# A four-layer sequence model: the first layer cut in two, its scan set beside two attentions, its preparation beside the last layers

## The chip, the core and the metric

One core of one Trainium2 chip. The metric is the device time of one execution in microseconds (us), lower is better. One core works through eight independent sequences of 512 rows by 128 columns, one after the other; nothing is exchanged with other cores. Engine names are those of the profile: PE (TensorE), DVE (VectorE), ACT (ScalarE), POOL (GpSimd), SP (SyncE, which here only issues transfers).

## The reference, cut to what matters

The input is x, eight sequences of 512x128 in float32. Each goes through four pairs of layers; a layernorm stands before each layer and a residual is added after it:

```python
# pair 0: a two-way selective scan (Mamba), then 16 experts of width 64, top 2 of 16 in groups
xc    = silu(causal_conv(xi))                    # 256 channels, forward and reversed
delta = softplus(dt @ dtproj_w.T + dtproj_b)
h     = exp(delta * A) * h + (delta * xc) * B    # over 512 positions, 16 states a channel
y     = ((h * C).sum(states) + D * xc) * silu(z) # both directions averaged, projected, added to x
# pair 1: attention, 16 heads of 64 with a relative bias, then 8 low-rank experts
# pair 2: attention, 16 heads of 8, rotary, causal; then a layer that begins with a second
#         16-head attention of 8 (rotary, not causal) and ends with 8 experts of width 512
# pair 3: a memory layer (8 recurrences), then 8 gated experts of width 256
```

The scan of one sequence is 2 directions x 2 halves of the channels x 16 states = 64 steps, each a first-order recurrence on a 128x512 tile.

## The kernel before, in words

All tiles are 128 partitions by 512 columns. Most stages are blocks with a barrier between them. The order of one pass (`layers`, L1495 to L2029) is: `moe0`, `attn1`, `lora1`, `attn2` (causal), `attn3`, and then the stage `slot`. Inside `slot` two streams share all engines: `mamba` (L669 to L958), which does the whole first layer of the **next** sequence, and `last_layers` (L1275), which does the rest of this one (ln1, experts 2, ln2, ln3, memory, ln4, experts 3). The first sequence's first layer runs alone in a stage `first`; the last pass (names that begin with z) has no first layer beside it. The passes but the last are one hardware loop (`Fori`) of seven.

How two streams are merged is written out by hand. Each stream is a generator per engine that yields a due time before each piece; `in_turn` (L583) always takes the stream with the earlier due time. So the order on each engine is fixed when the program is built, and an engine that waits for a semaphore holds back all that stands behind it, of both streams. The due times are only ranks; the true pace is set by the waits.

One scan step m is five instructions: PE broadcasts row B into a PSUM bank (L769, `DRIVE`, three banks), DVE multiplies it by `du` (L935), ACT makes the decay (L839), DVE scans (L942), POOL multiplies by row C (L859), PE adds the product into `SUM` (L777). SP loads row C, spread over the partitions, into one of three buffers (L726). In the order of DVE the product of step s stands ahead of the scan of step s-1:

```python
yield SCAN + STEP * s + 0.4
V.tensor_tensor(DRIVE[s % 3], DRIVE[s % 3], du[:, d, t, :], ALU.mult)          # step s
V.tensor_tensor_scan(work[:, m % RW, :], decay[m % RD], DRIVE[m % 3], 0.0, ...) # m = s - 1
```

What comes before the scan (norms, projection, convolution, softplus, rows B and C; L730 to L910) is called the preparation here. Its tiles and the scan's share SBUF.

A 16-head attention (`rope_attention`, `head8_attention`, L367 to L576, `project_back`) is: norm, projection, rotary and splitting into bf16 parts on DVE, then 93 steps in which PE makes the scores S of a tile (L426), DVE takes its row maximum (L550 causal, L553 not), and, 20 steps later, PE makes them again transposed (T), ACT takes the exponential (L524), POOL masks the diagonal in the causal one (L533), and PE weighs the values (L485). S and T tiles go through a ring of six PSUM banks (`RING`, L378), transposes and sums have banks 6 and 7 to themselves. All weights lie in SBUF (`WF`).

## Time and profile before

| | |
|---|---|
| median of 3 runs | 5811.86 us (5811.77 to 5815.04) |
| the profiled execution's own time | 5812.37 us |
| its span, first to last instruction | 5810.6 us |
| granted TensorE clock, mean over the span | 0.844 |
| busy share PE, DVE, ACT, POOL | 77%, 65%, 53%, 20% |

Busy time of an engine is counted once where its instructions overlap. The clock is the share of full speed that TensorE was granted: 0.5 is 1.2 GHz and 1.0 is 2.4 GHz. In a window row the engines stand in the order PE, PEld (weight loads), DVE, ACT, POOL. In a timeline or lines row what stands in brackets or behind the second bar is idle time of the engine just before, and what released it.

### The profile page before, as it was taken

To read this page: it belongs to the slowest core of one execution; us is meant where nothing else is said; L and a number is where in the kernel's file an instruction comes from. 1 tells how busy PE (TensorE), PEld (TensorE's weight loads), DVE (VectorE), ACT (ScalarE), POOL (GpSimd) and SP (SyncE) were. 2 spreads that over 40 slices of the span, in tenths; PEclk is the share of its full clock that TensorE was granted. 3 is DMA by queue.
4 is the path that set the end of the run, shared out by engine and by line. 5 is a ranking of instruction groups with operands and counts; after the bars stand their busy time and mean duration, and the time that the engine had idled before them with its cause. 6 is when DMAs were issued, how large, how long until landed. Compare 5 with 4: busy or idle time off the path is not lost. (4 is left out here: it accounts for less than half of the span.)

```text
span 5810.6 us, 67170 instructions
## 1 busy us (share of the span) xinstructions
PE 4485.7 (77%) x20516; PEld 2226.2 (38%) x20516; DVE 3772.0 (65%) x8877; ACT 3064.0 (53%) x5351; POOL 1140.3 (20%) x1356
## 2 busy tenths in 40 slices
PE   5786778877788777887778777788778877788777
PEld 2342434424344243442434324343243433444334
DVE  6756586565865658656686556865668555686554
ACT  3365645556455555555655556555565555555443
POOL 2401132011320123201231012310123111231100
PEclk8996989978898788987889878897789987899778
DMA  4210021100210002100121001210012100121000
GB/s 160 87 36 1 21 65 55 32 1 25 67 55 26 1 28 71 52 22 1 34 73 47 20 1 37 75 48 13 1 42 75 46 11 1 44 73 47 7 1 2
DMA packets 104076, 218.53 MB, mean 38 GB/s; under 512 B 11072, under 2 KB 19776, under 8 KB 103152
## 3 DMA queue, kind: packets, MB, share of 16 engines
q1 hardware_dynamic: 103680, 213.81, 11.6%
q8 instruction: 180, 2.95, 0.2%
q14 instruction: 216, 1.77, 0.1%
HBM read 211.08 MB, written 2.69 MB: 37 GB/s over the span
## 5 line engine op out<-in xcount | busy, mean ns | idle before, releaser
L859 POOL TENSOR_TENSOR slot_work<-slot_work,slot_c_all 128x512 f32<-128x512 f32 x448 | 570.2, 1273 | 1015.9 <-DVE slot_work L942 1015.0
L777 PE MATMUL BANKS<-slot_work,WF 128*128 128x512 f32 x896 | 530.5, 679 | 5.7 <-DVE slot_du L918 2.9
L524 ACT ACTIVATE attn_prob<-BANKS 128x512 f32<-128x512 f32 (+3 forms) x896 | 401.5, 532 | 122.5 <-PE BANKS L426 119.0
L1000 PEld LDWEIGHTS BANKS<-WF,slot_x_a 128*128 128x128 f32 x2688 | 359.3, 197 | 264.5 <-ACT slot_x_a L1040 133.5
L1000 PE MATMUL BANKS<-WF,slot_x_a 128*128 128x128 f32 x2688 | 373.3, 283 | 86.3 <-ACT slot_x_a L1040 86.3
L1010 PE MATMUL BANKS<-XT,WF 128*128 128x512 f32 x768 | 425.3, 639 | 2.6 <-ACT slot_comb_t L306 2.6
L769 PE MATMUL BANKS<-slot_bcs,WB 96*128 96x512 bf16 x448 | 189.1, 422 | 305.1 <-DVE slot_work L942 304.0
L202 POOL TENSOR_TENSOR rstd<-rstd,WF 128x4 f32<-128x4 f32 x40 | 40.3, 1007 | 1572.7 <-DVE rstd L220 1559.5
L1809 DVE CUSTOM_DVE_ANT_0 attn_biased<-BANKS,attn_toep 128x512 f32<-128x512 f32 x448 | 306.0, 684 | 51.9 <-PE BANKS L1707 46.6
L1788 ACT COPY attn_probt<-BANKS 128x512 f32<-128x512 f32 x448 | 261.0, 583 | 147.3 <-PE BANKS L1714 144.4
L426 PE MATMUL BANKS<-attn_parts_kT,attn_parts_qT 64*128 64x512 bf16 (+3 forms) x896 | 309.2, 437 | 33.6 <-ACT attn_parts_qT L504 20.7
L935 DVE TENSOR_TENSOR BANKS<-BANKS,slot_du 128x512 f32<-128x512 f32 x448 | 307.6, 687 | 36.0 <-PE BANKS L769 33.4
L942 DVE TENSOR_TENSOR_SCAN slot_work<-slot_decay,BANKS 128x512 f32<-128x512 f32 x273 | 329.7, 1208 | 0.0
L1780 ACT ACTIVATE attn_prob<-attn_biased,attn_nmax 128x512 f32<-128x512 f32 x448 | 326.9, 730 | 1.3 <-DVE attn_nmax L1809 1.2
L553 DVE TENSOR_REDUCE attn_nmax<-BANKS 128x1 f32<-128x512 f32 x448 | 282.0, 683 | 67.9 <-PE BANKS L426 65.6
L1714 PE MATMUL BANKS<-WF,attn_prob 128*128 128x128 f32 x1792 | 280.3, 281 | 7.6 <-ACT attn_probt L1788 4.3
L550 DVE CUSTOM_DVE_ANT_0 attn_masked<-BANKS,WF 128x128 f32<-128x128 f32 (+1 forms) x448 | 202.1, 489 | 127.4 <-PE BANKS L426 126.6
L1714 PEld LDWEIGHTS BANKS<-WF,attn_prob 128*128 128x128 f32 x1792 | 190.9, 140 | 243.9 <-DVE attn_prob L1816 157.0
L1707 PE MATMUL BANKS<-attn_qk 64*128 64x512 f32 x896 | 257.8, 653 | 4.7 <-ACT attn_qk L1762 4.7
L426 PE MATMUL BANKS<-attn_qm,attn_parts_kT 64*128 64x512 bf16 (+3 forms) x896 | 238.8, 394 | 17.1 <-ACT attn_qm L510 11.3
L1814 DVE RECIPROCAL attn_rden<-attn_den 128x1 f32<-128x1 f32 x448 | 72.1, 161 | 275.3 <-ACT attn_prob L1780 272.3
L485 PE MATMUL BANKS<-attn_prob,attn_vals 128*32 128x512 f32 (+3 forms) x1792 | 226.1, 580 | 16.9 <-ACT attn_prob L524 10.7
(674 smaller groups left out, 9464.7 us busy)
## 6 DMA issues: line engine op xcount, KB each, us to landing
slot_c_all<-c_rows SPq DMA_DIRECT2D x448, 256.0 KB, 3.1
attn_toep<-bias_line SPq DMA_DIRECT2D x112, 448.0 KB, 4.4
first_c_all<-c_rows SPq DMA_DIRECT2D x64, 256.0 KB, 3.1
WF<-in_wf SPq DMA_DIRECT2D x4, 1964.0 KB, 16.2
zattn_toep<-bias_line SPq DMA_DIRECT2D x16, 448.0 KB, 4.3
WF<-in_wf SPq DMA_DIRECT2D x3, 800.0 KB, 17.2
WF<-in_wf SPq DMA_DIRECT2D x3, 785.5 KB, 6.0
XIN<-in_x SPq DMA_DIRECT2D x8, 256.0 KB, 2.9
```

Source lines behind the costliest of these rows:

```text
L426: nc.tensor.matmul(bank(kind, i), left[rows, P * tile:P * (tile + 1)], right[rows, lo:hi], start=True, stop=True).then_inc(sem, 1)
L524: nc.scalar.activation(prob[:, i % PR, lo:hi], bank("T", i), ACT.Exp).then_inc(exped, 1)
L553: V.tensor_reduce(nmax[:, j, h:h + 1], bank("S", s), AX.X, ALU.max, negate=True).then_inc(maxed, 1)
L777: nc.tensor.matmul(SUM, ident, work[:, m % RW, :], start=(n == 0), stop=(n == NS - 1)).then_inc(acc, 1)
L859: nc.gpsimd.tensor_tensor(work[:, m % RW, :], work[:, m % RW, :], c_all[:, m % RC, :], ALU.mult).then_inc(rd, 1)
L935: V.tensor_tensor(DRIVE[s % 3], DRIVE[s % 3], du[:, d, t, :], ALU.mult).then_inc(drv, 1)
L942: V.tensor_tensor_scan(work[:, m % RW, :], decay[m % RD], DRIVE[m % 3], 0.0, ALU.mult, ALU.add).then_inc(scn, 1)
L1000: last = nc.tensor.matmul(DOWN[e % 2][:, j * D:(j + 1) * D], a1[:, i % 3, j * P:(j + 1) * P], w_down[:, i * D:(i + 1) * D], start=(t == 0 ...
L1010: last = nc.tensor.matmul(place("up", i), w_up[:, i * P:(i + 1) * P], XT[:, :], start=True, stop=True)
L1714: last = nc.tensor.transpose(bank[:, kt * P:(kt + 1) * P], prob[:, u % NP_, kt * P:(kt + 1) * P], ident)
L1780: nc.scalar.activation(prob[:, e % NP_, :], biased[:, e % NS_, :], ACT.Exp, bias=nmax[:, e:e + 1], scale=-1.0, accum_out=den[:, e:e + 1]). ...
L1809: V.tensor_tensor_reduce(biased[:, s % NS_, :], PS[s % NS_], toep[:, h % 4, c:c + SEQ], -1.0, BIG, ALU.add, ALU.min, nmax[:, s:s + 1]).the ...
```

## The change

- `mamba` becomes `mamba_pre` (the preparation) and `mamba_scan`. What passes between them (`M_KEPT`) lives in SBUF all the time; a tile `XM` takes the scan's result.
- The stages `attn2`, `attn3` and `slot` become two: `heads`, where the scan for sequence b+1 runs beside both 16-head attentions, and `last`, where the preparation for b+2 runs beside the last layers. The start is `p0`, `s0`, `p1`: preparation and scan of sequence 0, preparation of sequence 1, each alone. The loop is six passes, then a pass y (scan, no preparation) and a pass z (neither).
- The attentions become merged streams with due times (`rope_parts`, `head8_parts`, `back_parts`, which issue the same arithmetic). Banks 0 to 2 are the scan's; S, T and all transposes share a ring of four banks (3 to 6), taken in a fixed order, and bank 7 sums the weighed values.
- The scan has two `DRIVE` banks for three, four decay buffers for five, six work buffers for eight; each step's scan follows its own product. One step is due each 2.8 attention steps, from due time 4.0 (1.95 and alone in `s0`).
- The weights of experts 2 are no longer in SBUF: SP loads them expert by expert, 512 KB each, into a ring of three.
- `last_layers` copies `XM` to `X`; experts 3 have other due times (3.0 for 5.2).

```diff
     XTM = sbt(top, "XTM", [P, SEQ])
+    XM = sbt(top, "XM", [P, NJ, D])
+    M_KEPT = (sbt(top, "m_zs", [P, ND, SEQ]), sbt(top, "m_xc", [P, 2, ND, SEQ]), sbt(top, "m_delta", [P, 2, ND, SEQ]),
+              sbt(top, "m_du", [P, 2, ND, SEQ]), sbt(top, "m_bcs", [96, 2, SEQ], BF16))
...
-    def head8_attention(st, parts, vals, causal, O):
...
-        RING = 6
...
-    def mamba(st, after=None):
...
-        RD, RW, RC, AHEAD, FLUSH = 5, 8, 3, 5, 4
-        PRE, SCAN, STEP = 13.5, 52.0, 2.6
-        TAIL = SCAN + STEP * STEPS
...
+    def mamba_pre(st, fetch):
+        PRE = 13.5
+        zs, xc, delta, du, bcs = M_KEPT
...
-        SUM, DRIVE, OUT = PS[0], (PS[1], PS[2], PS[3]), PS[1]
...
         def sync(sp):
+            yield -3.0
+            sp.dma_start(XIN[:, :, :], fetch()).then_inc(xin_ld, 16)
...
+            yield 52.0
+            sp.wait_ge(cput, 32)
...
+    def mamba_scan(st, dest, START, STEP):
+        STEPS = 2 * ND * NS
+        RD, RW, RC, LATE = 4, 6, 3, 2
+        TAIL = START + STEP * STEPS
+        zs, xc, delta, du, bcs = M_KEPT
...
+        b_cast, dec, drv, scn, rd, acc = (st.sem(n) for n in ("b_cast", "dec", "drv", "scn", "multiplied", "acc"))
...
+        SUM, DRIVE, OUT = PS[0], (PS[1], PS[2]), PS[1]
...
+        def sync(sp):
+            for m in range(STEPS):
+                d, _, n = step(m)
+                yield at(m - 3)
+                if m >= RC:
+                    sp.wait_ge(rd, m - RC + 1)
+                row = c_dram[d, n:n + 1, :]
+                src = bass.AP(row.tensor, row.offset, [[0, P], [1, SEQ]])
+                sp.dma_start(c_all[:, m % RC, :], src).then_inc(c_ld[m % RC], 16)
...
+        def tensor(pe):
+            for s in range(STEPS + LATE):
+                if s < STEPS:
+                    d, _, n = step(s)
+                    yield at(s) - 1.0
+                    if s >= 2:
+                        pe.wait_ge(scn, s - 1)
+                    row = WBF("pick", 96)[:, n:n + 1]
+                    nc.tensor.matmul(DRIVE[s % 2], bc(row, [96, P]), bcs[:, d, :], start=True, stop=True).then_inc(b_cast, 1)
+                m = s - LATE
+                if m >= 0:
+                    n = m % NS
+                    yield at(s) + 0.45 * STEP
+                    pe.wait_ge(rd, m + 1)
+                    if n == 0 and m:
+                        pe.wait_ge(emptied, m // NS)
+                    nc.tensor.matmul(SUM, ident, work[:, m % RW, :], start=(n == 0), stop=(n == NS - 1)).then_inc(acc, 1)
...
+                d, t, n = step(m)
+                yield at(m - 2) + 0.3 * STEP
+                if m >= RD:
+                    act.wait_ge(scn, m - RD + 1)
+                a = (d * ND + t) * NS + n
+                nc.scalar.activation(decay[m % RD], delta[:, d, t, :], ACT.Exp, scale=W("A")[:, a:a + 1]).then_inc(dec, 1)
+        def gpsimd(pool):
+            for m in range(STEPS):
+                yield at(m) + 0.9 * STEP
+                pool.wait_ge(scn, m + 1)
+                pool.wait_ge(c_ld[m % RC], 16 * (m // RC + 1))
+                nc.gpsimd.tensor_tensor(work[:, m % RW, :], work[:, m % RW, :], c_all[:, m % RC, :], ALU.mult).then_inc(rd, 1)
...
-            for s in range(STEPS + 1):
-                yield SCAN + STEP * s + 0.4
-                if s < STEPS:
-                    d, t, n = step(s)
-                    dve.wait_ge(b_cast, s + 1)
-                    if s % (ND * NS) == 0:
-                        dve.wait_ge(dud, d + 1)
-                    V.tensor_tensor(DRIVE[s % 3], DRIVE[s % 3], du[:, d, t, :], ALU.mult).then_inc(drv, 1)
-                m = s - 1
-                if m >= 0:
...
+            for s in range(STEPS):
+                d, t, n = step(s)
+                yield at(s)
+                dve.wait_ge(b_cast, s + 1)
+                V.tensor_tensor(DRIVE[s % 2], DRIVE[s % 2], du[:, d, t, :], ALU.mult).then_inc(drv, 1)
+                if s >= NS and n == LATE:
+                    yield at(s) + 0.2 * STEP
                     flush(s // NS - 1)
-            yield TAIL + STEP * (AHEAD + 1) + 1.0
+                yield at(s) + 0.5 * STEP
+                dve.wait_ge(drv, s + 1)
+                dve.wait_ge(dec, s + 1)
+                if s >= RW:
+                    dve.wait_ge(acc, s - RW + 1)
+                V.tensor_tensor_scan(work[:, s % RW, :], decay[s % RD], DRIVE[s % 2], 0.0,
+                                     ALU.mult, ALU.add).then_inc(scn, 1)
+            yield TAIL + STEP * LATE + 1.0
             flush(2 * ND - 1)
...
-            V.tensor_tensor(X[:, :, :], XIN[:, :, :], OUT.rearrange(tiles, j=NJ), ALU.add)
+            V.tensor_tensor(dest[:, :, :], XIN[:, :, :], OUT.rearrange(tiles, j=NJ), ALU.add)
...
+        def sync(sp):
+            for e in range(E if stream is not None else 0):
+                yield at - 10.0 if e < RW else at + 0.2 + step * tiles_per * (e - RW + 1)
+                if e >= RW:
+                    sp.wait_ge(used, tiles_per * (e - RW + 1))
+                sp.dma_start(ring_w[:, e % RW, :], stream[e]).then_inc(w_ld[e % RW], 16)
...
                 yield at + 0.2 + step * i
-                last = nc.tensor.matmul(place("up", i), w_up[:, i * P:(i + 1) * P], XT[:, :], start=True, stop=True)
+                if stream is not None and i % tiles_per == 0:
+                    pe.wait_ge(w_ld[i // tiles_per % RW], 16 * (i // tiles_per // RW + 1))
...
+                                 FF // P, comb2, comb2_t, Y, 7.4, 2.0, stream=w2)
         ln2 = norm_parts(st, "ln2", Y, XN, SMALL, 73.0, gain=W("g2"), shift=W("be2_2"))
...
-                                 W("b2_3", E3), E3, HID // P, comb3, comb3_t, XO, 138.0, 5.2)
+                                 W("b2_3", E3), E3, HID // P, comb3, comb3_t, XO, 138.0, 3.0)
...
             nc.vector.tensor_tensor(XO[:, :, :], X[:, :, :], XN[:, :, :], ALU.add).then_inc(freed, 1)
+            if copy_next:
+                dve.wait_ge(freed, 1)
+                nc.vector.tensor_copy(X[:, :, :], XM[:, :, :])
             for layer in (ln3, memo, ln4, moe3):
...
+    def rope_parts(st, tag, ready, w_qkv, bias, half, tiles4, banks, at, again):
...
+    def head8_parts(st, tag, rope, tiles4, causal, O, ring, wbank, at, u):
...
+            return at + u * s
+        order = [("turn", n) for n in range(4)]
+        for s in range(N + LAG + 8):
+            if s < N:
+                order += [("S", s)] + [("turn", s)] * (4 <= s < H)
+            if s % PER == 2 and 1 <= s // PER <= NGR:
+                order.append(("Q", s // PER - 1))
+            if 0 <= s - LAG < N:
+                order.append(("T", s - LAG))
+            i = s - LAG - 7
+            if 0 <= i < N and i % PER == PER - 1:
+                order.append(("O", i // PER))
+        slot = {item: n for n, item in enumerate(order)}
+        done = {"S": maxed, "T": exped, "turn": ev, "Q": q_moved, "O": o_normed}
...
+        def tensor(pe):
+            def take(kind, i):
+                n = slot[kind, i] - len(ring)
+                if n >= 0:
+                    pe.wait_ge(done[order[n][0]], order[n][1] + 1)
+                return bank(kind, i)
...
+                    if causal:
+                        V.tensor_tensor_reduce(got, got, W("early")[:, SEQ - hi:], -1.0, BIG,
+                                               ALU.add, ALU.min, nmax[:, j, h:h + 1]).then_inc(maxed, 1)
+                    else:
+                        V.tensor_reduce(nmax[:, j, h:h + 1], got, AX.X, ALU.max, negate=True).then_inc(maxed, 1)
...
+    def back_parts(st, tag, heads, O, turned_o, w_o, add_to, banks, at, bias=None):
...
+    def both_attentions(st, at, u):
+        RING, WEIGH = PS[3:7], PS[7]
...
+        for tag, w_qkv, bias, half, causal, w_o, add_to, bias_o in (
+                ("a2", W("qkv2"), None, False, True, W("o2"), X, None),
+                ("a3", W("qkv3"), W("bqkv3"), True, False, W("o3"), XN, W("bo3"))):
+            ln = norm_parts(st, f"{tag}_ln", X, XN, SMALL, at, dst_t=XT, banks=(RING[1], RING[0]), after=before)
+            rope = rope_parts(st, tag, ln.ready, w_qkv, bias, half, raw, RING, at + 6.0, bool(layers))
+            head = head8_parts(st, tag, rope, heads, causal, O, RING, WEIGH, at + 26.0, u)
+            back = back_parts(st, f"{tag}_pb", head, O, ot[:, 0, :], w_o, add_to, RING, head.end + 0.5, bias=bias_o)
+            layers += [ln, rope, head, back]
+            at, before = head.end + 4.5, (back.added, 1)
...
-    with Stage("first", last=True) as st:
-        layer = mamba(st)
+    with Stage("p0") as st:
+        layer = mamba_pre(st, lambda: one(xs, 0))
         with nc.Block() as block:
             run(block, layer)
...
+    with Stage("s0") as st:
+        layer = mamba_scan(st, X, 2.0, 1.95)
+        with nc.Block() as block:
+            run(block, layer, clear=True)
+        release_stale()
+    with Stage("p1", last=True) as st:
+        layer = mamba_pre(st, lambda: one(xs, 1))
+        with nc.Block() as block:
...
+    def layers(b, scan_next, pre_next):
...
-        def rope_attention(st, w_qkv, bias, half, causal, O):
...
-        def project_back(st, tag, O, w_o, add_to, bias=None):
...
-        with Stage("slot", last=True, at_end=store) as st:
-            taken = st.sem("x_taken")
-            streams = [mamba(st, after=(taken, 1))] if ahead else []
-            streams.append(last_layers(st, taken))
+        with Stage("heads", last=True) as st:
+            streams = [mamba_scan(st, XM, 4.0, 2.8)] if scan_next else []
...
+            streams.append(both_attentions(st, 0.0, 1.0))
             with nc.Block() as block:
-                run(block, *streams, first=clear)
...
-    with nc.Fori(0, out.shape[0] - 1) as b:
-        layers(b, True)
+        with Stage("last", last=True, at_end=store) as st:
+            streams = [mamba_pre(st, lambda: one(xs, b + 2))] if pre_next else []
+            streams.append(last_layers(st, scan_next))
+            with nc.Block() as block:
+                run(block, *streams)
+    n = out.shape[0]
+    with nc.Fori(0, n - 2) as b:
+        layers(b, True, True)
+    prefix[0] = "y"
+    layers(n - 2, True, False)
     prefix[0] = "z"
-    layers(out.shape[0] - 1, False)
+    layers(n - 1, False, False)
```

## Rows read from the trace of the kernel before

**Rows 1.** The page: busy time and share of each engine; costliest group, line 859

```profile
PE 4485.7 (77%) x20516; PEld 2226.2 (38%) x20516; DVE 3772.0 (65%) x8877; ACT 3064.0 (53%) x5351; POOL 1140.3 (20%) x1356
L859 POOL TENSOR_TENSOR slot_work<-slot_work,slot_c_all 128x512 f32<-128x512 f32 x448 | 570.2, 1273 | 1015.9 <-DVE slot_work L942 1015.0
```

**Rows 2.** Windows by stage: from:to, length, busy and count per engine, clock, DMA, GB/s

```profile
225.60:424.00 198.40, 175.90 (x860) 92.56 (x860) 118.59 (x366) 115.83 (x253) 19.09 (x13) 0.92 0.13 39
424.00:613.40 189.40, 132.09 (x784) 50.65 (x784) 111.00 (x327) 98.83 (x204) 28.61 (x80) 0.72 0.00 1
613.40:940.50 327.10, 247.04 (x912) 132.71 (x912) 240.44 (x412) 174.04 (x217) 95.27 (x76) 0.87 0.17 53
5623.50:5807.50 184.00, 141.61 (x668) 91.17 (x668) 84.57 (x217) 58.31 (x85) 4.04 (x4) 0.84 0.00 1
```

**Rows 3.** Windows, the two 16-head attentions of the first pass in five pieces

```profile
424.00:447.00 23.00, 7.65 (x20) 4.03 (x20) 12.59 (x31) 7.04 (x17) 4.35 (x6) 0.57 0.01 1
447.00:509.90 62.90, 51.16 (x360) 18.93 (x360) 34.28 (x154) 37.32 (x87) 18.26 (x64) 0.74 0.00 1
509.90:539.80 29.90, 11.57 (x37) 6.76 (x37) 15.56 (x39) 6.61 (x14) 6.01 (x10) 0.56 0.00 1
539.80:569.30 29.50, 27.03 (x138) 9.96 (x136) 23.18 (x44) 16.73 (x30) 0.00 (x0) 0.59 0.00 1
569.30:609.00 39.70, 32.83 (x228) 9.41 (x226) 23.32 (x50) 31.13 (x58) 0.00 (x0) 0.99 0.00 1
```

**Rows 4.** Timeline, VectorE in the scan by itself: start, length, engine, line, operation

```profile
208.04 0.67 DVE L935 TENSOR_TENSOR BANKS<-BANKS,first_du 128x512 f32<-128x512 f32 x1
208.62 1.21 DVE L942 TENSOR_TENSOR_SCAN first_work<-first_decay,BANKS 128x512 f32<-128x512 f32 x1
209.74 0.67 DVE L935 TENSOR_TENSOR BANKS<-BANKS,first_du 128x512 f32<-128x512 f32 x1
```

**Rows 5.** Windows, four stretches of the first stage "slot", first layer and last layers together

```profile
613.40:692.80 79.40, 62.48 (x264) 37.83 (x265) 47.91 (x110) 48.14 (x61) 10.86 (x9) 0.86 0.04 11
722.00:757.00 35.00, 19.61 (x52) 8.54 (x51) 29.90 (x62) 14.19 (x22) 10.86 (x9) 0.68 0.15 48
815.00:860.00 45.00, 34.78 (x95) 16.64 (x94) 33.47 (x64) 20.05 (x25) 15.14 (x13) 0.83 0.21 68
860.00:924.00 64.00, 57.53 (x215) 31.02 (x215) 56.47 (x84) 47.11 (x52) 29.94 (x24) 1.00 0.28 89
```

**Rows 6.** Windows, experts alone in the last pass; lines, their gelus within 613.4:692.8

```profile
5631.00:5693.90 62.90, 60.89 (x336) 43.91 (x335) 13.80 (x50) 24.08 (x35) 0.00 (x0) 0.96 0.00 1
L1040 ACT ACTIVATE slot_x_a<-BANKS,WF 128x512 f32<-128x512 f32 x22 | 14.7, 686 | 19.0 <-PE BANKS L1010 18.8
```

**Rows 7.** Timeline, the first VectorE instruction after two stage ends; in brackets the idle time

```profile
225.57 0.68 DVE L215 BATCH_NORM_STATS2 stats<-X 128x6 f32<-128x128 f32 x3 [1.88 <-PEq L136]
940.55 0.68 DVE L215 BATCH_NORM_STATS2 stats<-X 128x6 f32<-128x128 f32 x3 [6.93 <-issue]
```

**Rows 8.** Windows, the first layer alone at the start: preparation, then 64 scan steps

```profile
51.30:101.00 49.70, 23.17 (x39) 6.85 (x39) 34.93 (x65) 20.36 (x25) 7.43 (x7) 0.78 0.01 2
101.00:214.40 113.40, 82.42 (x185) 27.30 (x185) 113.28 (x134) 45.66 (x64) 82.05 (x64) 0.91 0.47 148
```

**Rows 9.** Lines, VectorE at 722:760 beside the scan, and at 5693.9:5724 without it

```profile
L1235 DVE TENSOR_TENSOR slot_mu<-slot_root 128x64 f32<-128x64 f32 x1 | 0.9, 949 | 0.0
L1212 DVE TENSOR_TENSOR slot_qkv<-slot_qkv,slot_parts 128x512 f32<-128x512 f32 x4 | 2.6, 683 | 0.0
L1235 DVE TENSOR_TENSOR zslot_mu<-zslot_root 128x64 f32<-128x64 f32 x1 | 0.2, 224 | 0.0
```

**Rows 10.** The page, DMA issues: tensor, count, KB each, median us to landing

```profile
attn_toep<-bias_line SPq DMA_DIRECT2D x112, 448.0 KB, 4.4
WF<-in_wf SPq DMA_DIRECT2D x3, 785.5 KB, 6.0
XIN<-in_x SPq DMA_DIRECT2D x8, 256.0 KB, 2.9
```

838 lines of the change are left out of this document (412 added, 426 removed).

## The prediction

> **What bounds the kernel now.** I read the page first: DVE 65% and PE 77% of the span, neither full [rows 1]. So the span is a chain of stages with different limits, and the windows by stage are the view that counts [rows 2]. One pass is 198.4 us up to `lora1`, which the change leaves alone, 189.4 us for the two 16-head attentions and 327.1 us from there to the next pass, the stage `slot` with its end. The same last layers without the first layer beside them take 184.0 us. The reader should compare DVE in the four rows: 111.0 us busy of 189.4 in the attentions, 240.4 of 327.1 in `slot`. The scan brings most of the latter: by itself it keeps DVE full (113.28 of 113.40 us) and costs 1.70 us a step, 209.74 less 208.04 [rows 4, 8], so 64 steps are 109 us of DVE wherever they stand. The change moves them to where DVE has 78 us free in 189 and must lengthen that stage, and shortens the other.
>
> **Stage `heads`, with the scan.** Due times place the steps: step s is due at 4+2.8s, an attention's first S at 26, its last step at 119, the second attention's first S at 149.5. That gives 8 scan steps before the first S, 33 in the first attention's steps, 11 between, 12 in the first 34 steps of the second, and none after due time 183. The five pieces of the attentions alone are rows 3. To each I add its scan steps at 1.70 us of DVE:
>
> - before S: 12.6 + 13.6 = 26.2 us of DVE in a piece that took 23.0;
> - first attention: 34.3 + 56.6 = 90.9, took 62.9;
> - between (back projection, norm, rotary): 15.6 + 18.6 = 34.2, took 29.9;
> - first third of the second: 23.2 + 20.5 = 43.7, took 29.5.
>
> Together 195 us of DVE work in pieces that take 145 us now. No engine is ever quite full in a merged stretch, so the question is the share. Three stretches of `slot` bound it: 85% in the norms and splitting of 722 to 757, 74% in 815 to 860, where norm, gate and logits form a chain, and 88% at 860 to 924, where PE was 90% busy too [rows 5]. I take 80% for the two serial pieces (33 and 42 us) and 85 to 88% for the two attention pieces (107 and 49.5 us): 231.5 us, 84% overall. PE comes close but is not the bound: the scan by itself has PE busy 82.4 us in 64 steps, 1.29 each [rows 8]; with the attention's own 51.2 us the largest piece has 94 us of PE at the lower clocks of 0.74 and 0.91, inside 107. ACT has 37 + 24 and POOL 18 + 42 there (0.71 and 1.27 us a step [rows 1, 8]), both covered.
>
> Then the second attention's rest as now, 39.7 us [rows 3], plus 2 for three or four flushes of the sum and the output product that fall there; 3.5 us for the back projection (4.4 now, to 613.4); 2 us for the stage's end, as after `first`, where DVE sat idle 1.88 us [rows 7]. **`heads` is 279 us.** The barriers between the old blocks go, a gain that I leave inside the shares; the smaller ring of four banks I price at nothing in the rest: DVE was busy only 23.3 of those 39.7 us, and the binding engine is PE with 32.8. If PE waits for the older bank more often there, it costs at most one row maximum per four steps, some 9 us of 39.7.
>
> One rule speaks against putting the scan here. DVE work with both inputs in SBUF slows down beside POOL: the small product of line 1235 took 949 ns beside the scan and 224 without [rows 9]. Each rotary part has ten such products and subtractions, and the POOL multiplication that can hold them lasts 1.27 us [rows 1]. At 19 scan steps in the two serial pieces the worst case is 19 x 1.27 = 24 us a pass. Line 1235 lost 0.7 us, while four subtractions of the rotary part's kind (line 1212) kept 683 ns beside the same scan [rows 9]; so I count 2 to 3 us per serial piece, inside the 80%. The Trainium skill ("SBUF — State Buffer", section "Who interferes with whom") says that a DVE instruction with two SBUF inputs and a GpSimd instruction that reads SBUF lock each other out for the whole instruction, whichever starts first. By that rule, the trace agrees for line 1235; that every scan step hits one is the fourth rival.
>
> **Stage `last`, with the preparation.** Until 692.8 the stage `slot` is just this: preparation beside experts 2. In those 79.4 us 22 of 32 tiles had their gelu [rows 5, 6]. Ten remain at 62.9/32 = 1.97 us, 19.7; about 1.5 us of the 79.4 was the scan's beginning. So 97.5 us to the end of experts 2. The rest alone is 5807.5 less 5693.9 = 113.6 us, the copy of X 0.5, and the loop's end 6.9 us of idle DVE [rows 7]. **218.5 us**, against 327.1. The streamed weights: 512 KB lie between the transfers of 448 KB in 4.4 us and of 785.5 KB in 6.0 [rows 10], so about 4.7; a ring of three gives each load the time of some eight tiles, 16 us, and it is hidden. Only the first could be late: it is issued behind XIN (2.9 us) at the stage's start and lands after 7.6 us if alone, and in the last pass the experts began 7.5 us into the stage, at 5631.0 [rows 6]. I cost it at nothing; if the first three loads share the engines it lands with the third, 3 x 4.7 + 2.9 = 17 us in, up to 9.5 us late. SP's waits for rows B and C stand ahead of the loads of experts 6 and 7, which have the same slack. The other due times of experts 3 have no stream to be ranked against.
>
> **The start.** `p0` must now fetch XIN itself: 2.9 + 0.5. `s0` has each scan right behind its own product. They no longer overlap in DVE's pipe: between 0.67 + 1.21 = 1.88 without and 1.70 with full overlap [rows 4] the next product still overlaps the scan before it, so 1.85 a step, 64 x 0.15 = 9.5 us more. A barrier, about 1 us. `p1` is a new 49.7 us of preparation [rows 8], with 3.4 for XIN, 2.5 until POOL's last `du`, and 1 of barrier. Together **70 us** lost once.
>
> **The sum**, against the profiled execution's 5812.4 us (span 5810.6, some 1.8 around it; the median 5811.9 is 0.5 below):
>
> - six loop passes: 189.4 + 327.1 - 279 - 218.5 = 19.0 us each, gain 114;
> - the seventh, with no preparation: 516.5 becomes 279 + 184.0 + 6.9, gain 46.6;
> - the last pass: attentions in one block, gain 3;
> - the start: loss 70.
>
> Net gain 93.5, so 5719; against the median the same within a microsecond. I predict **5720**.
>
> What decides is `heads`. It counts seven times; one microsecond there is 7 us of the time, and the gain is gone at 279 + 93.5/7 = 292.4 us, that is when the shared stretches keep DVE busy below 195/245 = 80%. That is not far from 84%.
>
> **The rivals.** (1) *Tighter overlap*: nothing but exponentials and copies on ACT in `heads`, and PE brought to a higher clock by the scan's matmuls where it now runs at 0.56 to 0.59 [rows 3]. DVE at 93% makes the shared part 210 us, `heads` 257, the time 5720 - 154 = 5566. For it: `slot` already has 88% with PE equally loaded. Against: four banks instead of six.
>
> (2) *The order holds DVE back; slower than before.* PE is two steps ahead of DVE at most: S of step s+2 waits for the maximum of step s, in one queue with the scan's broadcast, its sum and the bursts of eight value products. Each time such a burst falls between two S, DVE runs dry, and the next scan product stands behind the row maximum that is late. At the 74% of 815 to 860 [rows 5] the shared part is 262 us, `heads` 310, the time about 5935. It decides from 80% down, where `heads` passes 292 us.
>
> (3) *The streamed weights arrive late*, the first by 9.5 us in all eight passes and a later one by 1.5: 88 us, 5808, no change. For it only the order on SP's queue; against it the sizes above.
>
> (4) *POOL holds DVE back* for a whole multiplication on every scan step in the serial pieces: 24 - 5 = 19 us a pass more than counted, 5720 + 133 = 5853. For it line 1235, against it line 1212 [rows 9]. The page of the Trainium skill named above would have it wherever the two meet.
>
> That the change doesn't do what it says has one form: the scan is not over midway but its steps lag, since due times are only ranks. It would not; ranks fix the order, and 12 steps before the 34th S is certain.
>
> **Chances.** Forecast 0.55, its own range 5660 to 5790; rival 1 0.20; rival 2 0.17; rival 3 0.05; rival 4 0.03. The range reaches to `heads` of 262 us below, 5600, and 296 us above, 5835; outside lie half of rival 1 and most of rival 2. A difference of 0.2%, 12 us, is about what can be told from no change here. Faster by more: the forecast, rival 1 and a little of the rest, 0.77. Within: 0.04. Slower: rivals 2 and 4 and the forecast's edge, 0.19.
>
> **What would show it.** In the changed profile: windows from the first norm of the attentions to the stage's end of 279 us with DVE about 83% busy and the scan's last step some 225 us in; scan steps 3.1 to 3.4 us apart in the first attention; from there to the next pass 218 us, with the end of experts 2 near 97; `s0` at 1.85 us a step; no idle PE that a weight transfer ends; first `moe0` norm at about 295 us. The prediction is wrong if `heads` exceeds 292 us, or if `last` misses 218 by more than 10.

## The result, and the profile after

| | before | after |
|---|---|---|
| median (runs) | 5811.82 us (4) | 5903.35 us (4, 5894.45 to 5915.09) |
| the profiled execution's own time | 5812.37 us | 5915.09 us |
| its span | 5810.6 us | 5913.4 us |
| ratio of the times, 95% interval | | 1.0159 [1.0139, 1.0179] |

The changed kernel is slower by 91.5 us, 1.6%. 5720 us had been predicted, a gain of 1.6%; 5903 lies 68 us above the range. One of the six executions of a later variant (the scan at two rates) fell in a slow state, 6089.5 us at a granted clock of 0.764 where its others had 0.855 to 0.857, and stands in none of the figures below.

The page of the kernel after, its busy row, the product by row C and the streamed weights:

```profile
PE 4554.5 (77%) x20516; PEld 2170.7 (37%) x20516; DVE 3845.2 (65%) x8884; ACT 2729.6 (46%) x5086; POOL 1115.4 (19%) x1324
L714 POOL TENSOR_TENSOR heads_work<-heads_work,heads_c_all 128x512 f32<-128x512 f32 x384 | 495.9, 1291 | 648.5 <-DVE heads_work L747 647.0
last_x_w<-in_w SPq DMA_DIRECT2D x48, 512.0 KB, 3.5
```

Against [rows 1] the shares of PE and DVE are the same, and nothing shows where the time went. DVE has 73 us more to do in all, though the change adds next to no work to it. ACT has 334 us less: its table loads fall from 385 to 120, which is 494 and 154 us in the two traces, and no stage became shorter by that. So one goes to the stages. The windows of the first pass, `heads`, then `last` in two parts, up to the end of experts 2 and from there:

```profile
497.20:798.70 301.50, 225.62 (x992) 77.43 (x992) 241.39 (x463) 141.16 (x268) 106.93 (x140) 0.82 0.20 60
798.70:898.60 99.90, 81.86 (x380) 52.66 (x380) 50.74 (x121) 50.33 (x66) 10.85 (x9) 0.88 0.11 35
898.60:1020.50 121.90, 79.28 (x324) 45.69 (x324) 67.42 (x156) 34.61 (x50) 3.02 (x3) 0.79 0.01 3
```

`heads` took 301.5 us where 279 was predicted, `last` 221.8 where 218.5 was. Together 523.3, while the kernel before needs 516.5 for the same work [rows 2]. The six loop passes have a mean of 301.7 in `heads` and 221.3 in `last`. The same windows, `heads` cut at the first S of the first attention, its last output, the first S of the second, the last scan step, and the last output:

```profile
497.20:537.50 40.30, 21.28 (x52) 8.57 (x53) 34.26 (x49) 15.70 (x31) 15.49 (x14) 0.58 0.23 68
537.50:641.90 104.40, 91.74 (x449) 30.11 (x447) 94.53 (x225) 57.33 (x116) 58.06 (x97) 0.93 0.27 80
641.90:688.60 46.70, 26.24 (x76) 11.31 (x76) 40.81 (x63) 15.03 (x28) 18.21 (x18) 0.71 0.23 72
688.60:734.20 45.60, 39.84 (x153) 11.93 (x153) 42.47 (x67) 20.35 (x35) 13.91 (x11) 0.81 0.18 54
734.20:787.90 53.70, 44.70 (x252) 14.12 (x252) 26.64 (x55) 32.18 (x58) 1.27 (x1) 0.90 0.00 1
787.90:798.70 10.80, 1.81 (x12) 1.39 (x12) 2.68 (x12) 0.59 (x1) 0.00 (x0) 0.81 0.32 107
```

Set the first five against the five of [rows 3]. The four rows that hold scan steps add up to 237.0 us, with DVE busy 212.1: 89.5%. The prediction had 231.5, with 195 busy: 84%. So DVE was used better than forecast and had more to do. The fifth row, called the rest from here on, has the attention's work of the last row of [rows 3], 39.7 us, and takes 53.7, with every engine waiting part of the time. No scan step starts in it, but the scan's tail lies there: the last two sums and the output product on PE (20 of its 252 matmul records), and four instructions on DVE. The sixth is the end of the stage; its timeline on DVE:

```profile
790.63 0.69 DVE L1512 TENSOR_TENSOR XN<-XN,BANKS 128x512 f32<-128x512 f32 x1 [2.05 <-PE BANKS L1492]
797.32 0.87 DVE L412 BATCH_NORM_STATS2 mstats<-XIN 128x6 f32<-128x128 f32 x4 [6.00 <-DMA XIN<-in_x]
798.72 0.86 DVE L412 BATCH_NORM_STATS2 stats<-XN 128x6 f32<-128x128 f32 x4
```

DVE stands idle 6.00 us until the next sequence has landed. That load is issued when the stage begins, and the preparation's norm, which reads it, stands ahead of the layer's own norm in DVE's order. The kernel before loads it long ahead.

Two parts came out as forecast. The first `moe0` norm starts at 297.9 (295 predicted). And in `s0` DVE takes 1.85 us a step, as predicted (148.44 to 150.28 is one step):

```profile
148.44 0.67 DVE L738 TENSOR_TENSOR BANKS<-BANKS,m_du 128x512 f32<-128x512 f32 x1
149.15 1.22 DVE L747 TENSOR_TENSOR_SCAN s_work<-s_decay,BANKS 128x512 f32<-128x512 f32 x1
150.28 0.67 DVE L738 TENSOR_TENSOR BANKS<-BANKS,m_du 128x512 f32<-128x512 f32 x1
```

### The profile page after: what moved, and what is told of

The parts are those of the page before. It is cut to its first block and busy times, and to the rows that moved or that the text cites. A ratio compares the mean times of both kernels' runs of the same rounds, so it can differ in the third digit from the quotient of the medians.

```text
span 5913.4 us, 66181 instructions
## 1 busy us (share of the span) xinstructions
PE 4554.5 (77%) x20516; PEld 2170.7 (37%) x20516; DVE 3845.2 (65%) x8884; ACT 2729.6 (46%) x5086; POOL 1115.4 (19%) x1324
## 5 line engine op out<-in xcount | busy, mean ns | idle before, releaser
L714 POOL TENSOR_TENSOR heads_work<-heads_work,heads_c_all 128x512 f32<-128x512 f32 x384 | 495.9, 1291 | 648.5 <-DVE heads_work L747 647.0
L691 PE MATMUL BANKS<-heads_work,WF 128*128 128x512 f32 x768 | 505.0, 744 | 82.5 <-POOL heads_work L714 69.9
L1426 ACT ACTIVATE heads_prob<-BANKS 128x512 f32<-128x512 f32 (+3 forms) x768 | 375.8, 523 | 346.8 <-PE BANKS L1323 342.3
L738 DVE TENSOR_TENSOR BANKS<-BANKS,m_du 128x512 f32<-128x512 f32 x512 | 359.1, 701 | 101.1 <-PE BANKS L683 98.5
L1453 DVE TENSOR_REDUCE heads_nmax<-BANKS 128x1 f32<-128x512 f32 x384 | 249.4, 680 | 88.4 <-PE BANKS L1323 88.4
L1323 PE MATMUL BANKS<-heads_parts_kT,heads_parts_qT 64*128 64x512 bf16 (+3 forms) x768 | 241.2, 377 | 78.7 <-DVE heads_nmax L1453 54.5
L683 PE MATMUL BANKS<-m_bcs,WB 96*128 96x512 bf16 x512 | 226.7, 443 | 96.0 <-DVE heads_work L747 57.3
L1450 DVE CUSTOM_DVE_ANT_0 BANKS<-BANKS,WF 128x384 f32<-128x384 f32 (+3 forms) x512 | 245.0, 493 | 62.4 <-PE BANKS L1323 62.0
L1323 PE MATMUL BANKS<-heads_qm,heads_parts_kT 64*128 64x512 bf16 (+3 forms) x768 | 221.2, 365 | 18.7 <-DVE heads_nmax L1450 10.5
L747 DVE TENSOR_TENSOR_SCAN heads_work<-heads_decay,BANKS 128x512 f32<-128x512 f32 x192 | 233.2, 1215 | 2.1
```

What stands on the lines that cost most here:

```text
L691: nc.tensor.matmul(SUM, ident, work[:, m % RW, :], start=(n == 0), stop=(n == NS - 1)).then_inc(acc, 1)
L714: nc.gpsimd.tensor_tensor(work[:, m % RW, :], work[:, m % RW, :], c_all[:, m % RC, :], ALU.mult).then_inc(rd, 1)
L738: V.tensor_tensor(DRIVE[s % 2], DRIVE[s % 2], du[:, d, t, :], ALU.mult).then_inc(drv, 1)
L747: V.tensor_tensor_scan(work[:, s % RW, :], decay[s % RD], DRIVE[s % 2], 0.0, ALU.mult, ALU.add).then_inc(scn, 1)
L1323: nc.tensor.matmul(take(kind, i)[:, lo:hi], left[rows, P * tile:P * (tile + 1)], right[rows, lo:hi], start=True, stop=True).then_inc(sem, 1)
L1426: nc.scalar.activation(prob[:, i % PR, lo:hi], bank("T", i)[:, lo:hi], ACT.Exp).then_inc(exped, 1)
```

## The experiments

Each starts from the kernel after, but for the second. "Halves" are the two halves of `heads`: from the first norm statistic of the first attention to that of the second, and from there to the first of the last layers; the mean of the six loop passes of the profiled run. "Last pass" is the same stage in pass z, which has no scan. One execution of the kernel after can differ from another by 10 us, so where a run stands alone the halves say more than its time.

| run | time, us | ratio to before | halves, us | stage | last pass |
|---|---|---|---|---|---|
| after | 5903.4 | 1.0159 | 149.2 + 152.5 | 301.7 | 203.2 |
| ring of 7, last pass | 5905.3 (one) | | 150.7 + 152.0 | 302.7 | 185.6 |
| load of XIN early | 5882.5 | 1.0122 [1.0101, 1.0142] | 149.3 + 148.8 | 298.1 | 203.4 |
| POOL, one column | 5827.1 (one) | | 142.2 + 147.3 | 289.5 | 203.6 |
| maximum into SBUF | 5889.0 (one) | | 148.0 + 150.8 | 298.8 | 203.0 |
| scan at 3.4 | 5847.5 (one) | | 136.1 + 155.8 | 291.9 | 203.3 |
| scan at 2.3 | 5915.5 (one) | | 169.7 + 132.8 | 302.5 | 203.6 |
| 7 banks from step 48 | 5852.7 | 1.0073 [1.0057, 1.0090] | 149.7 + 145.7 | 295.4 | 185.9 |
| all repairs, 3.4 | 5811.5 | 1.0002 [0.9985, 1.0019] | 134.3 + 150.2 | 284.5 | 183.5 |
| all, two rates | 5836.3 | 1.0052 [1.0039, 1.0065] | 129.3 + 163.8 | 293.1 | 184.5 |
| all, 3.6 | 5868.7 | 1.0098 [1.0084, 1.0113] | 135.4 + 162.7 | 298.1 | 183.9 |
| all, ring of 5 | 5893.7 | 1.0150 [1.0133, 1.0167] | 146.5 + 154.5 | 301.0 | 183.4 |

My theory after the result: the term priced at nothing, the ring of four banks, costs some 12 us in the rest; the load costs 6; POOL most of what remains. The rival: the merged order itself, or DVE and the matmuls together, set the pace everywhere.

**Seven banks in the last pass.**

```diff
-        RING, WEIGH = PS[3:7], PS[7]
+        RING, WEIGH = PS[0:7] if wide else PS[3:7], PS[7]
```

`wide` is set where no scan lies beside the attentions.

> The kernel after, with one change in the last pass alone, where no scan lies beside the two attentions: their ring takes seven banks of PSUM instead of four. Theory A (a ring of four banks holds the attentions back, the term that I priced at nothing): this stage falls from the 203.2 us of the kernel after to 187 to 193, the 189.4 of the kernel before, and the time falls by 10 to 16 us. Theory B (it is the order in which the two attentions are now written, or the maximum that is written back into its bank): the stage stays within 3 us of 203.2. A value between, 194 to 200, says that both carry a part. Nothing else in the program changes: the seven stages with a scan stay at 300 to 303 us.

The two halves of that stage, first in the kernel after, then with seven banks:

```profile
5522.00:5623.00 101.00, 70.03 (x392) 26.76 (x392) 54.67 (x189) 46.24 (x104) 22.74 (x70) 0.62 0.00 1
5623.00:5725.20 102.20, 75.15 (x392) 25.55 (x392) 62.37 (x129) 55.49 (x100) 3.03 (x6) 0.75 0.00 1
```

```profile
5527.30:5618.90 91.60, 60.67 (x392) 25.30 (x392) 53.32 (x188) 44.94 (x104) 22.57 (x70) 0.69 0.00 1
5618.90:5712.90 94.00, 67.09 (x392) 24.28 (x392) 61.26 (x130) 53.41 (x100) 3.03 (x6) 0.75 0.00 1
```

203.2 becomes 185.6: theory A, and 1.4 us beyond the end of its range. The counts are the same; PE is busy 17.4 us less (145.2 and 127.8 over both halves), and the granted clock in the first half is 0.69 where four banks had 0.62. So some of what the ring costs may come by way of the clock; the runs don't part the two. The merged order with seven banks is even a little faster than the kernel before (189.4). The run's own time is 10 us under the kernel after's profiled execution (5915.1) and not 17, since its first `heads` happened to take 307.0 us; a single time can't carry 17 us here.

**Four banks in the kernel before.**

```diff
-        RING = 6
+        RING = 4
```

> The kernel before, with the ring of score banks in its two 16-head attentions cut from six banks to four and nothing else. There the attentions have no scan beside them in this place, and keep two more banks of their own for the turns. Theory A (the ring of four is what costs): the two attentions of each pass together, 189.4 us in the kernel before, grow by 6 to 14 us, the time by 45 to 110 us over eight passes. Theory B (the number of banks does not matter; the maximum in place or the merged order does): they stay within 2 us, the time within 15 us of the kernel before.

It took 5929.1 us (one run), 118 more than the kernel before and 8 beyond the range. The two attentions of the second pass, first in the kernel before, then with four banks:

```profile
1141.30:1232.80 91.50, 62.11 (x392) 25.69 (x392) 48.27 (x189) 44.96 (x104) 22.56 (x70) 0.69 0.00 1
1232.80:1330.30 97.50, 69.98 (x392) 25.19 (x392) 62.82 (x138) 53.89 (x100) 6.01 (x10) 0.75 0.00 1
```

```profile
1156.30:1257.00 100.70, 71.82 (x392) 26.90 (x392) 49.44 (x189) 46.41 (x104) 22.51 (x70) 0.60 0.00 1
1257.00:1358.30 101.30, 72.41 (x392) 24.58 (x392) 63.60 (x138) 55.56 (x100) 6.02 (x10) 0.77 0.00 1
```

189.0 becomes 202.0, close to the kernel after's 203.2 in the last pass, with no merged order and no maximum in place. One number of the old kernel gives the whole loss of the last pass: the ring costs 13 us here and 15 in the mean of the eight passes (118 by 8). Both experiments meet from two sides, so this is shown for attentions without a scan beside them. Of the 13 us, 9 lie in the first attention; how much is left where a scan lies beside them, these two runs can't tell.

**The load of the next sequence, behind the end of the scan.**

```diff
+            sp.wait_ge(put, 1)
+            sp.dma_start(XIN[:, :, :], fetch()).then_inc(xin_in, 16)
+            sp.wait_ge(xin_in, 16)
```

These lines stand in `mamba_scan`, behind the load of the last row C; `put` says that the scan's result is in `XM` and XIN free.

> The kernel after, with the load of the next sequence moved from the start of the last layers into the stage before, behind the end of the scan, where the scan has read the old one for the last time. My account of the kernel after: VectorE stands idle 6.0 us at the start of each of the six stages of last layers with a preparation, until that load lands, because the preparation's first statistic stands ahead of the layer's own norm in VectorE's order. Then each of the six becomes 4.5 to 6 us shorter and the time falls by 27 to 36 us, to 5865 to 5880 by the kernel after's 5903: still slower than the kernel before, by 0.9 to 1.2%. Rival: the load only covers an idle start that the norm's own chain would have had anyway, and less than 2 us of the 6 come back (time within 12 us of the kernel after).

The same place on DVE:

```profile
785.28 0.69 DVE L1519 TENSOR_TENSOR XN<-XN,BANKS 128x512 f32<-128x512 f32 x1 [2.05 <-PE BANKS L1499]
788.52 0.87 DVE L412 BATCH_NORM_STATS2 mstats<-XIN 128x6 f32<-128x128 f32 x4 [2.55 <-PEq L139]
```

The idle time falls from 6.00 to 2.55 us, not to nothing: 2.55 is the end of the stage, which the load had covered. Six times 3.45 is 21, and 21 us is what the median time fell by. The mechanism was right; the expectation (27 to 36) had forgotten what lies under a wait.

**POOL's product on one column.** All scans leave out the product by C but for one column.

```diff
-    nc.gpsimd.tensor_tensor(work[:, m % RW, :], work[:, m % RW, :], c_all[:, m % RC, :], ALU.mult)
+    nc.gpsimd.tensor_tensor(work[:, m % RW, 0:1], work[:, m % RW, 0:1], c_all[:, m % RC, 0:1], ALU.mult)
```

> The kernel after, with GpSimd's product by C in every step of the scan cut to one column of 512 (it leaves that product out for the other 511 columns, in all the scans). It separates what GpSimd's presence takes from the rest of what the scan costs. If GpSimd's 1 us operations hold VectorE's two-operand and copying instructions up where they overlap, the short serial pieces of the stage with the scan lose their stretched instructions (in the kernel after 3.55 us for a group that takes 1.11 alone, 1.6 for 0.68): the first piece falls from 40.3 to 32 to 37 us, the third from 46.7 to 42 to 45, and the stage from 301.5 to 287 to 296. If GpSimd's product is instead the pace of the scan itself, the large attention pieces (104.4 us) would fall by over 5 us too. Rival: neither holds, and the stage stays at 299 to 303 us, since VectorE and the matmuls set it.

Four windows of the first pass, cut at the first S of the first attention, the first norm statistic of the second, and its first S; then the same of the kernel after, whose first window stands above:

```profile
497.10:533.10 36.00, 21.38 (x53) 8.49 (x53) 29.62 (x49) 15.63 (x31) 6.87 (x14) 0.61 0.23 80
533.10:640.80 107.70, 93.97 (x469) 33.13 (x467) 97.72 (x230) 59.46 (x119) 24.55 (x98) 0.95 0.27 84
640.80:678.80 38.00, 21.79 (x57) 8.86 (x57) 32.20 (x59) 13.15 (x25) 5.35 (x16) 0.69 0.20 69
678.80:789.30 110.50, 86.93 (x417) 27.64 (x417) 71.06 (x131) 53.10 (x93) 2.27 (x12) 0.86 0.11 33
```

```profile
537.50:646.40 108.90, 96.17 (x469) 32.66 (x467) 98.80 (x230) 59.19 (x119) 60.22 (x98) 0.93 0.27 82
646.40:688.60 42.20, 21.80 (x57) 8.77 (x56) 36.54 (x58) 13.16 (x25) 16.05 (x16) 0.68 0.22 66
688.60:798.70 110.10, 86.36 (x417) 27.44 (x417) 71.78 (x131) 53.11 (x93) 15.18 (x12) 0.86 0.11 33
```

The serial pieces lose 4.3 and 4.2 us, the attention pieces 1.2 and nothing. The same number of instructions keeps DVE busy 34.26 and 29.62 us in the first: what goes is waiting inside instructions. The rotary part's subtraction, line 1259, 497 to 540 us, with the full product and with one column:

```profile
L1259 DVE TENSOR_TENSOR heads_rot<-heads_rot,heads_parts_q 128x512 f32<-128x512 f32 x2 | 2.3, 1165 | 0.1
```

```profile
L1259 DVE TENSOR_TENSOR heads_rot<-heads_rot,heads_parts_q 128x512 f32<-128x512 f32 x2 | 1.4, 692 | 0.1
```

With the full product one of the two takes 1.64 us and the other 0.69; over the whole stage of this pass three of the line's eight are long, without it none. POOL's product costs 8.5 us in the serial pieces of this pass, and the whole stage 12 us in the mean of six. In part that is clock: in the second pass the first attention, from its first maximum to its last output, takes 103.9 us at a granted clock of 0.93 with the product and 101.3 at 0.97 without. That DVE waits here is the rule of the Trainium skill ("SBUF — State Buffer", section "Who interferes with whom") on DVE and GpSimd instructions that lock each other out, and the trace agrees for this line. The attention pieces of this pass, where DVE mostly reads PSUM, are all but spared.

One long wait stays with the product cut: the four instructions of the norm at the head of the stage. With them stands what POOL does meanwhile in the kernel after; last comes the same norm in the kernel before:

```profile
499.82 3.55 DVE L424 TENSOR_SCALAR XN<-X,mv,rstd 128x128 f32<-128x128 f32 x4 [1.12 <-POOL rstd L396]
499.74 1.32 POOL L1174 MEMSET heads_vals<- 128x1472 f32 x1
502.41 0.82 POOL L1178 MEMSET heads_parts_k<- 128x832 bf16 x1
426.75 1.11 DVE L226 TENSOR_SCALAR XN<-X,mv,rstd 128x128 f32<-128x128 f32 x4 [1.12 <-POOL rstd L202]
```

Five fills of the attention's tiles, lines 1174 to 1178, keep POOL busy from 499.74 to 503.23, just as long as DVE stands in line 424. In the kernel before they begin at 429.12, behind the norm. The merged order has moved them beside it, at 2.4 us or more a pass, the last one included. No run moves the fills back, so this is read from the times alone.

**The maximum's result into SBUF.**

```diff
-  V.tensor_tensor_reduce(got, got, W("early")[:, SEQ - hi:], -1.0, BIG, ...)
+  V.tensor_tensor_reduce(masked[:, s % 2, 0:hi], got, W("early")[:, SEQ - hi:], -1.0, BIG, ...)
```

> The kernel after, with the causal maximum's elementwise result written to a tile of two slots in SBUF, as the kernel before has it, and not back into the bank of PSUM that it read. The read of the accumulator behind each of the 64 maxima takes 136 to 141 ns in the kernel after and 83 in the kernel before; if the place of the result is the cause it returns to 83, and VectorE has 3.6 us less to do in each first attention. Where VectorE sets the pace (the shared pieces of the first attention, 94.5 us busy of 104.4) 2 to 4 us a pass come back, in the last pass without a scan 0 to 2 of 101.0: the time falls by 12 to 30 us. Rival: PE and the ring of four set the pace there, and the time stays within 10 us of the kernel after's 5903.

The read of the accumulator, in the kernel after and here:

```profile
L1450 DVE DVE_READ_ACCUMULATOR2_ANT heads_nmax<- x64: 136/139/146, 537.7 to 616.4; 128x1 f32 x64
```

```profile
L1452 DVE DVE_READ_ACCUMULATOR2_ANT heads_nmax<- x64: 81/82/86, 535.7 to 611.5; 128x1 f32 x64
```

The place of the result sets it: 139 and 82 ns. The last pass does not change, as expected. The first half becomes 1.2 us shorter where 2 to 4 were expected, and the second half, which the edit doesn't touch, is 1.7 us shorter too, so the effect on the stage can't be told from the spread of the passes. The one time is 14 us under the kernel after's median but only 5 under the lowest of its four, so it doesn't decide between the theory and its rival.

**The rate of the scan.**

```diff
-            streams = [mamba_scan(st, XM, 4.0, 2.8)] if scan_next else []
+            streams = [mamba_scan(st, XM, 4.0, 3.4)] if scan_next else []     # and 2.3
```

> The kernel after, with one scan step to 3.4 attention steps instead of 2.8, so that the scan is over near the end of the second attention and not midway in it. In the first attention six or seven scan steps fewer stand beside it: VectorE's 94.5 us of 104.4 there fall by 10. Theory A (VectorE is the bound of the shared pieces, and stands idle in half of the rest alone, 26.6 of 53.7 us busy): the first attention's half of the stage falls from 149 to 141 to 144 us, the second half grows from 152 to 152 to 156, the stage with the scan to 294 to 299 from 301.5, the time by 15 to 50 us. Theory B (the matmuls and the ring of four set the pace wherever the attention runs, so scan steps cost the same wherever they lie): the stage stays at 300 to 304.

> The kernel after, with one scan step to 2.3 attention steps instead of 2.8: the scan is over before the second attention has well begun. The counterpart of the run at 3.4. Theory A: the first half of the stage grows from 149 to 155 to 160 us (eight scan steps more of about 1.5 us of VectorE each), the second falls from 152 to 143 to 147, and the stage is at 300 to 306, the time within 30 us of the kernel after, on the slower side. Theory B: the stage stays at 300 to 304 with both halves little changed.

The halves of the second pass, at 3.4, at 2.8 (the kernel after) and at 2.3:

```profile
1211.60:1348.30 136.70, 106.22 (x497) 37.86 (x497) 119.29 (x262) 71.01 (x143) 66.35 (x105) 0.84 0.22 71
1348.30:1504.70 156.40, 118.27 (x497) 38.66 (x495) 120.19 (x204) 71.37 (x125) 40.42 (x36) 0.83 0.18 54
```

```profile
1221.20:1369.80 148.60, 116.52 (x520) 40.95 (x520) 133.18 (x276) 74.86 (x150) 75.55 (x112) 0.84 0.25 78
1369.80:1522.30 152.50, 108.26 (x473) 36.27 (x472) 108.38 (x189) 66.28 (x118) 31.25 (x28) 0.81 0.14 42
```

```profile
1221.10:1392.70 171.60, 134.42 (x546) 46.94 (x547) 149.51 (x298) 81.20 (x159) 86.71 (x121) 0.81 0.26 82
1392.70:1524.80 132.10, 94.04 (x447) 32.92 (x445) 90.46 (x168) 61.42 (x109) 19.78 (x19) 0.81 0.10 31
```

POOL's counts tell the scan steps: 70 of the first half's are masks and the like (the last pass has 70 without a scan), so it holds 35, 42 or 51, and the second half the other 29, 22 or 13. Against the last pass's 101 us, 35 steps cost 35 us by the means of the table, 1.0 each; the next seven 1.9 each, the next nine 2.3. In the second half going from 13 to 22 steps costs 2.2 each, the tail of the scan included, and from 22 to 29 only 0.5. A step is 1.9 us of DVE work. Where DVE is full it costs more than that, where it has room it costs half or less, and 2.8 puts it in the dearest place for 42 of the 64. Theory A, and stronger than expected (5847 against 5853 to 5888, the first half 136 against 141 to 144). At 2.3 the first half was dearer still (170 against 155 to 160) and the second cheaper.

**What the rest is made of.** The run at 2.3 also parts the ring from the scan's tail, since there the scan's result is written at 725.1, before the rest begins. All five rows run from the 35th row maximum of the second attention to its last output: the kernel before with six banks; the kernel after with four in the last pass, without a scan; the run at 2.3 with four in its first pass; the kernel after in its first and in its sixth pass:

```profile
569.40:607.20 37.80, 31.89 (x222) 8.77 (x220) 22.53 (x49) 30.44 (x57) 0.00 (x0) 1.00 0.00 1
5677.00:5719.50 42.50, 35.87 (x231) 9.98 (x231) 22.91 (x50) 31.96 (x58) 0.00 (x0) 1.00 0.00 1
744.00:786.50 42.50, 35.88 (x231) 9.97 (x230) 22.92 (x50) 32.13 (x58) 0.00 (x0) 1.00 0.00 1
735.30:788.00 52.70, 44.31 (x251) 13.94 (x251) 25.64 (x54) 31.85 (x57) 0.23 (x1) 0.90 0.00 1
4358.10:4407.70 49.60, 41.19 (x251) 12.38 (x249) 25.60 (x54) 31.85 (x57) 0.19 (x1) 0.97 0.00 1
```

Four banks for six cost 4.7 us, in the pass without a scan and behind one that is over (the kernel before, cut to four banks, takes 42.1). The other 10.2 come only where the tail lies in the rest: 20 matmul records more, PE busy 8.4 us longer, and a granted clock of 0.90 where the others have 1.00. Where it is 0.97 the tail costs 7.1. So the larger part of the loss in the rest is the tail and not the ring, against my theory.

**Three repairs, with seven banks from step 48 on.** `head8_parts` gives the second attention's tiles banks 0 to 6 from the first free slot at step 48; the first use of banks 0 to 2 waits for the scan's result.

```diff
+            if more is not None and wide_at is None and s >= more[0] and len(order) % len(ring) == 0:
+                wide_at = len(order)
...
+                elif held[n] < 3:
+                    pe.wait_ge(*more[1])
```

> Three repairs together: the load of the next sequence behind the end of the scan (as in the run before), seven banks for the ring in the last pass, and, in the seven passes with a scan, seven banks for the second attention from its step 48 of 93 on, where the scan has given its three banks back. The first two measured alone gave 21 us and, in the stage of the last pass, 17.6. If the ring of four is what holds the rest of the stage back, the second attention of each pass with a scan becomes 3 to 6 us shorter, and the sum is 5903 less 21, 17 and 21 to 42: 5823 to 5844. Rival: in the rest the second attention is held by ScalarE's exponentials or by the order in which the steps are written, the seven passes gain under 1 us each, and the time is 5860 to 5870.

5852.7 us, 9 above the range and 7 below the rival's. The second half is 145.7, against 148.8 with the load alone: 3.1 a pass. Part of that is chance, for in both runs passes differ in their granted clock; in passes whose first third of the second attention took the same time, the rest takes 51.0 for 52.7 us, at a clock of 0.90 in both. That is 1.7 a pass, as is the time: 5882.5 less 17.6 and seven times 1.7 is 5853. So the ring does hold the rest with a scan before it, but giving the banks back late recovers only 1.7 of the 4.7 us.

**All repairs.** Rate 3.4, the early load, seven banks in the last pass, the maximum into SBUF; then the variants.

```diff
-            return START + STEP * s
+            return START + SLOW * min(s, TURN_AT) + STEP * max(s - TURN_AT, 0)
...
-        SUM, DRIVE, OUT = PS[0], (PS[1], PS[2]), PS[1]
+        SUM, DRIVE, OUT = PS[0], (PS[1], PS[1] if dest is XM else PS[2]), PS[1]
...
-        RING, WEIGH = PS[3:7], PS[7]
+        RING, WEIGH = PS[0:7] if wide else PS[2:7], PS[7]
```

The first pair is the run at two rates, the other two are the ring of five, each cut to its main lines.

> The repairs that were measured one by one, together: one scan step to 3.4 attention steps, the load of the next sequence behind the end of the scan, seven banks for the ring in the last pass, the causal maximum's result in SBUF. If they are independent (each acts in its own place: the first attention's shared stretch, the start of the last layers, the last pass) the sum is 5847.5 less 21, 17.6 and 14, that is 5795, between 5783 and 5807, and so just under the kernel before's 5811. Rival: the gains overlap (at 3.4 VectorE is no longer the bound of the first attention, so the shorter read of the accumulator gives nothing, and the scan now ends just before the stage does, so that the load is late again): 5815 to 5825, no faster than the kernel before.

> As the run with all repairs, but the scan at two rates: its first 52 steps at one to 3.9 attention steps, the last 12 at one to 2.0, so that more of them lie where the second attention has no scores left to reduce. From the runs at 2.3, 2.8 and 3.4 a scan step costs about 1.7 us where it lies in the first attention's half of the stage and 0.6 to 1.6 in the second. Between four and five steps move from the first half to the second: if these prices hold the stage becomes 1 to 5 us shorter, and the time is 8 to 35 us under that of the run with all repairs. Rival: VectorE, free of scores there, waits for the matmuls and the exponentials in a chain (scan, GpSimd's product, sum), the scan's tail then ends after the attention's, and the time is 0 to 40 us above that run.

> As the run with all repairs, with one scan step to 3.6 attention steps from an earlier start, so that the scan is spread over the whole stage. Two steps leave the first half at 1.7 us each and cost 0.6 to 1.6 in the second, where the scan's tail (the last sum, the product by the output matrix, the sum with the old sequence) now ends some 4 us behind the attention. Theory of the prices alone: the time is within 15 us under that of the run at 3.4. Rival, the tail shows: 10 to 35 us over it. Either way it tells where the best rate lies.

> As the run with all repairs at 3.4, with a fifth bank for the attentions' ring, which the scan gives up: its row of B is spread into one bank instead of two in turn, so that this matmul waits for the scan of the step just before it and not for the one before that. From four to six banks was worth 14.7 us a pass in the kernel before, without a scan beside it. Theory A, the ring still sets the pace at 3.4: the seven stages with a scan become 3 to 7 us shorter each, and the time is 5760 to 5795, under the kernel before. Rival: TensorE, which runs its instructions in order and was up to two scan steps ahead of VectorE, is now held at each of the 64 spreads until VectorE has finished the scan before it, the scores behind it come late, and what the fifth bank gives is lost: the stages stay as they are or grow by up to 20 us, the time is 5810 to 5950.

All repairs together: 5811.5 us in the median of 12 runs, equal to the kernel before, and between the range of independent gains (up to 5807) and the rival's (from 5815). The profiled run (5784.2) lies in the first of these ranges, but the twelve times reach from 5781 to 5835, far more than the kernel before's 5798 to 5816. The passes of the profiled run show how one kernel can do this: `heads` takes 281 to 282 us in four of seven and 289 to 290 in three. The first attention's piece in the first and the second pass:

```profile
523.00:630.70 107.70, 90.53 (x473) 32.27 (x472) 96.56 (x231) 62.89 (x126) 56.54 (x95) 0.91 0.25 76
1227.00:1338.50 111.50, 96.26 (x473) 33.06 (x471) 96.99 (x230) 62.57 (x125) 56.54 (x95) 0.84 0.25 73
```

The instructions are the same and DVE is busy the same, but the granted clock is 0.91 and 0.84 of full speed, PE is busy 5.7 us longer and the piece takes 3.8 us more; the second attention adds as much. What sets the clock of a pass stays open.

Two rates and 3.6: the first half falls by 5.0 us at two rates (four to five steps fewer) and not at all at 3.6, the second grows by 13.6 and 12.5 us. In the second pass at two rates the last row maximum starts at 1462.4 and the last layers' norm at 1500.1, 37.7 us later; at 3.4 it is 1461.8 and 1491.6, 29.8. The scan's result is written at 1492.2 and 1480.2. So the rival holds: the scan's end, a chain through DVE, POOL and PE, then shows behind the attention. Both are slower than 3.4, by 25 us, as the rival had it, and by 57, which is 22 beyond the rival's 10 to 35.

Ring of five: the rival, at 5893.7. Who waited for whom in the first `heads`, with five banks and with four:

```profile
PEld BANKS L691 <- DVE heads_work L755: 73.6, 47, 5.2
```

```profile
PEld BANKS L690 <- DVE heads_work L754: 19.1, 13, 3.7
```

PE's wait for the scan before the next spread of B grows from 19 to 74 us in a stage, and it stands in front of the scores. The bank gained is worth less than the freedom lost.

## Why the prediction was wrong

Against the profiled executions the sum missed by 195.8 us (5915.1 for 5719.3). By its own steps:

- **`heads`, 279 for 301.7**: 136 us over six passes, and 17 in pass y (296.3). This is the step that failed, and in it most of all the second attention's rest, "as now, 39.7", plus 2 for the scan's end: 41.7 for 53.7.
- **The last pass's attentions**, 186.4 for 203.2: 17 us, by the ring alone.
- **`last`**, 218.5 for 221.3: 17 us over six passes; 3 given back in pass y (190.9 for 187.7).
- **The start**, 70 for 72.3: right, step pace and all.
- Some 9 us are spread over the stages left alone.

Inside `heads` the terms of the first pass:

| piece | predicted | measured |
|---|---|---|
| before S, and between | 33 + 42 | 40.3 + 46.7 |
| first attention, first third of the second | 107 + 49.5 | 104.4 + 45.6 |
| the rest | 41.7 | 53.7 |
| back projection and stage end | 5.5 | 10.8 |

1. **The rest** holds two mis-sized terms. The scan's end was priced at 2 us, as a few instructions; it costs 10.2 where the clock is 0.90 and 7.1 where it is 0.97. Its matmuls stand in PE's queue between the scores: in the first pass DVE waits 4.72 us for the next score while PE is at the output product. And "the smaller ring of four banks I price at nothing in the rest": it costs 4.7 there, within the bound of "some 9" that the same sentence gave, and 15 to 17 over both attentions where no scan lies beside them, which the last pass had to pay and the sum left out. The argument for nothing was that DVE was busy only 23.3 of 39.7 us. But a ring isn't paid for in busy time of the engine that empties it: it sets how far PE may run ahead.
2. **XIN was not priced in `last`**, though the same text priced it at 3.4 in `p0` and `p1`. It shows with 6.0 us, of which 3.45 could be had back, 21 us of the time. The missed question was when the old XIN is read for the last time: that is at the end of the scan now, so the load could no longer be early.
3. **POOL at 2 to 3 us a serial piece**: 4.3 and 4.2 shown. The worst case of 24 (rival 4) is too much, the 5 too little. Another 2.4 us are the norm beside POOL's fills, which nothing in the text has. The two measure 10.9; the serial pieces took 12.0 more than the 75 of the forecast.
4. **DVE's work was under-counted.** The scan step stood in `heads` at 1.70 us, in `s0` at 1.85, for the same order of the same two instructions. 64 times 0.15 is 9.6, an estimate, since the pace was measured in `s0` alone. POOL's 10.8 (DVE busy 241.4 for 230.6 in the stage) is measured. The two are more than the 17.1 us between 195 and 212.1. The serial pieces also hold nine and twelve steps, not eight and eleven (18 and 24 instructions more than in [rows 3]).
5. **The shares of 80 to 88% were too careful**: 89.5% over the shared pieces. More work at a better share gives 237.0 for 231.5. That the two attention pieces came out near their forecast is luck: two errors offset each other.

What was right: the break-even of `heads` at 292.4 us. It came to 301.7 in six passes and 296.3 in the seventh, which by that step is 60 us of loss (6 x 9.3 + 3.9); the other terms above add some 43, together the 102.7 between the profiled executions. Rival 2 was nearest in number (5935), but its mechanism, DVE starved to 74% in the shared stretches, did not occur. No weight was late (rival 3: 3.5 us to landing).

That 2.8 is a poor rate was not looked at. It explains no part of the miss against the prediction, which had the same rate, but at 3.4 `heads` alone is 291.9, at the break-even. With the repairs the cut into two halves comes level with the kernel before and no version tried beats it. Left open: how the 10.2 us of the tail part between its matmuls and the lower clock, and what the ring of four costs in the stretches that hold scan steps, since the run with five banks changed the scan's order as well.

## What to carry to other kernels

When work is moved into a stage, count the buffers it takes from its host and price their loss by cutting the host's ring in the old kernel first: one constant changed gave the whole loss of the last pass here. Price the moved work's end by where it will stand in the host's queues: one run that moves it elsewhere tells it from the buffers. Price a moved step by place and density, not by its length: the same step cost 0.5 to 2.3 us. And of each tile that the moved work reads, ask when it is now free, since its next load moves along.

## What the runs showed of the hardware that I had not expected

- The read of the accumulator behind a VectorE maximum takes 139 ns where the elementwise result goes to PSUM and 82 where it goes to SBUF.
- The same stage of the same kernel (all repairs), in one execution, takes 281 or 290 us from pass to pass. The piece with its first attention had a granted clock of 0.91 in the first pass (282) and 0.84 in the second (290). Its twelve times spread over 0.9%, the kernel before's seventeen over 0.3%.
- DVE's subtractions of line 1259, on tiles that POOL doesn't touch, took 1.64 us three times in eight and 0.69 otherwise; without POOL's product beside them all eight took 0.69. The profile counts the waiting as busy time.
- Four short DVE instructions that take 1.11 us took 3.55 while POOL filled other tiles (1174 to 1178).
